# Token layers of a hybrid network: where the first two pairs of the second attention are prepared inside the experts before it

## What is computed

```python
t = t + _L2_attn_ref(_ln_t(t), ...)   # six heads of 16, softmax, the diagonal masked
t = t + _L2_ffn_ref(_ln_t(t), ...)    # four experts 96 -> 384 -> 96, gelu, a gate keeps the best two
t = t + _L3_attn_ref(_ln_t(t), ...)   # six heads of 16, causal
t = t + _L3_ffn_ref(_ln_t(t), ...)    # four experts again
```

## Time and profile before

| | us |
|---|---|
| median of 3 runs | 917.91 |
| lowest and highest | 914.95, 918.13 |
| the profiled execution, its own time | 918.22 |
| span of the profiled execution in the trace | 916.5 |
| PE busy, of the span | 792.8 (86%) |
| ACT busy, of the span | 487.9 (53%) |
| DVE busy, of the span | 548.3 (60%) |
| first experts, parts 6 and 7, on PE | 543.67 to 591.86 |
| first body of the second attention starts on PE | 596.11 |

### The profile page before, as it was taken

How to read it: one execution, slowest core, us unless ns; L and a number is a source line. 1 busy time by engine, 2 the same in 40 slices (tenths; PEclk the granted TensorE clock), 3 DMA queues, 4 the chain that set the end, 5 groups by cost and what they waited for, 6 DMA issues and landing times.

```text
span 916.5 us, 18605 instructions
## 1 busy us (share of the span) xinstructions
PE 792.8 (86%) x6130; PEld 656.2 (72%) x6130; DVE 548.3 (60%) x1632; ACT 487.9 (53%) x777; POOL 320.2 (35%) x365
## 2 busy tenths in 40 slices
PE   1898996899447999889999999789888799999997
PEld 1666664889325677667999998666666688888886
DVE  4799994553626688884555655445777644444442
ACT  0366665111324877775555655447777655555553
POOL 2211112910131444354333344514553553333332
PEclk9999995899758999999999999959999999999999
DMA  4750000000034554510000000344646000000000
GB/s 87 131 101 8 0 0 1 1 0 0 1 79 102 111 112 90 109 22 1 1 1 0 0 0 9 80 94 100 120 92 123 8 1 10 9 9 9 9 9 18
DMA packets 27570, 38.01 MB, mean 41 GB/s; under 512 B 9288, under 2 KB 24352, under 8 KB 27424
## 3 DMA queue, kind: packets, MB, share of 16 engines
q1 hardware_dynamic: 27520, 37.36, 19.7%
HBM read 25.06 MB, written 12.29 MB: 41 GB/s over the span
## 4 chain that ended last, share of the span: by engine, by line
PE 51%; ACT 8%; DVE 5%; DMA 4%; issue 3%; POOL 1%; SPq 1%; ACTq 0%; DVEq 0%; POOLq 0%
PE ps L1331 18%; PE ps L1323 13%; DMA keys<-at_parts 3%; PE ps L1148 3%; PE ps L1170 3%; PE ps L1186 3%; PE ps L1163 2%; ACT at_qs L1456 2%; DVE at_mf L1605 2%; ACT at_pT L1452 2%; PE ps L1213 2%; PE ps L1165 1%; PE ps L1310 1%; PE ps L1192 1%; SPq L1018 1%
## 5 line engine op out<-in xcount | busy, mean ns | idle before, releaser
L1516 ACT ACTIVATE ff_h<-ps,b 128x512 f32<-128x512 f32 x192 | 128.6, 687 | 116.2 <-PE ps L1323 115.8
L1331 PE MATMUL ps<-w,ff_h 128*128 128x96 f32 x1536 | 181.9, 275 | 6.7 <-ACT ff_fT L1522 6.7
L1331 PEld LDWEIGHTS ps<-w,ff_h 128*128 128x128 f32 x1536 | 178.5, 192 | 11.3 <-issue 8.4
L1720 DVE SCALAR_TENSOR_TENSOR tok<-ps,ff_gate,tok 128x96 f32 (+1 forms) x224 | 56.0, 311 | 121.1 <-PE ps L1331 117.0
L1605 DVE TENSOR_REDUCE at_mf<-ps 128x4 f32<-128x1024 f32 (+2 forms) x96 | 100.3, 1081 | 28.1 <-PE ps L1165 27.9
L1058 POOL TENSOR_SCALAR_AFFINE_SELECT at_pT<-at_pT 128x768 f32<-128x768 f32 x64 | 65.8, 1030 | 146.0 <-ACT at_pT L1452 145.4
L1452 ACT ACTIVATE at_pT<-ps 128x1024 f32<-128x1024 f32 (+2 forms) x96 | 87.0, 917 | 22.8 <-PE ps L1170 20.3
L618 DVE SCALAR_TENSOR_TENSOR ca_qk<-ps,dw,ca_qk 96x225 f32<-96x225 f32 (+1 forms) x256 | 97.6, 447 | 2.0 <-ACT ca_qk L467 2.0
L1163 PE MATMUL ps<-keys,at_qs 96*128 96x256 bf16 (+1 forms) x384 | 73.2, 276 | 29.4 <-DMA keys<-at_parts 19.8
L1323 PE MATMUL ps<-ff_xh,ff_wh 96*128 96x512 f32 x192 | 79.7, 415 | 1.3 <-DVE tok L1626 0.9
L1323 PE MATMUL ps<-ff_xh,ff_wl 96*128 96x512 f32 x192 | 75.4, 393 | 0.0
(11 more groups left out here) (231 smaller groups left out, 1529.9 us busy)
## 6 DMA issues: line engine op xcount, KB each, us to landing
at_parts<-at_part SPq DMA_DIRECT2D x96, 96.0 KB
at_qs<-at_parts SPq DMA_DIRECT2D x16, 288.0 KB, 4.3
keys<-at_parts SPq DMA_DIRECT2D x16, 288.0 KB, 5.3
at_qs<-at_parts SPq DMA_DIRECT2D x16, 192.0 KB, 5.8
keys<-at_parts SPq DMA_DIRECT2D x16, 192.0 KB, 6.2
w<-in_L_ffn_w SPq DMA_DIRECT2D x4, 576.0 KB
chan<-in_x SPq DMA_DIRECT2D x4, 384.0 KB, 5.5
at_qs<-at_parts SPq DMA_DIRECT2D x16, 96.0 KB, 6.5
```

Of the source, the lines that this page charges most:

```text
L1331: ins = nc.tensor.matmul(ps[:, 6 + e % 2, C * t:C * (t + 1)], h[:, e % 2, j, P * t:P * (t + 1)], L.f.w2[:, e * HC + j, :], start=(j == 0), ...
L1516: nc.scalar.activation(h[:, e % 2, j, :], ps[:, 3 * (e % 2) + j, :], ACT.Gelu, bias=L.f.b1[:, e * HC + j:e * HC + j + 1]).then_inc(f_h, 1)
```

## The change

The preparation of pairs 8 and 9 moves forward inside parts 6 and 7, on five lists:

- POOL normalises pair 8 in part 5, pair 9 in part 6 and pair 10 in part 7 (`first_experts`), each one part earlier, and ahead of that part's `low` and biases.
- PE transposes the pair after the first `hidden` of its part, into bank 7, once the last `expert` of the part before has left that bank. `queries_keys` stands before `turn_tokens` instead of before the last `result`. There is one more wait, on `s_xT` before `result` of expert 1, which writes bank 7.
- ACT copies `xT` between the gelus of expert 0 and 1. At the end of the part, `high` stands ahead of `tokens_high`, and `middle` of the same pair ahead of the gate's exponential.
- DVE does `rests` before the addition of expert 2 and `lows` before that of expert 3, in the same part.
- SP's list is the same. Its semaphores come earlier.

```diff
@@ POOL
+                def first_experts():
+
+                    part_(L2, 0, True, None)
+                    with pool.Fori(1, PAIRS - 3) as i:
+                        part_(L2, i, True, None)
+                    part_(L2, PAIRS - 3, True, L3.first)
+                    part_(L2, PAIRS - 2, True, L3.first + 1)
+                    part_(L2, PAIRS - 1, False, L3.first + 2)
@@ PE, rest_of_part and part_
                     hidden(L, i, 2)
+                    if pair:
+                        pe.wait_ge(s_xT, pair + 1)
                     result(L, i, 1)
                     hidden(L, i, 3)
                     pe.wait_ge(f_h, i * EH + 3 * HC + 1)
+                    if pair:
+                        queries_keys(L3, pair, pair % 2, qk_bank(pair))
                     if ahead:
                         turn_tokens(i + 1)
-                    if pair == L3.first:
-                        turn(pair, 1)
                     elif pair:
-                        turn(pair, 0)
                         values(L3, pair - 1, 0)
                     result(L, i, 2)
                     if ahead:
                         gate_products(L, i + 1)
-                    if pair:
-                        queries_keys(L3, pair, pair % 2, qk_bank(pair))
                     result(L, i, 3)
...
                     hidden(L, i, 0)
+                    if pair:
+
+                        pe.wait_ge(f_ac, i * E + 2)
+                        turn(pair, 7)
                     hidden(L, i, 1)
@@ ACT, next_part and part_
                     if pair:
-                        normed(pair, pair % 2, 1 if pair == L3.first else 0)
+                        high(pair, qk_bank(pair))
                     if ahead:
                         tokens_high(i + 1)
                     if pair == L3.first + 1:
                         values(pair - 1, 0)
+                    if pair:
+                        middle(pair)
                     if ahead:
                         nc.scalar.preload_act_table(ACT.Exp)
                         gate_exponential(i + 1)
                         nc.scalar.preload_act_table(ACT.Gelu)
-                    if pair:
-                        high(pair, qk_bank(pair))
...
-                        if e == 0 and pair == L3.first + 1:
-                            middle(L3.first)
+                        if e == 0 and pair:
+                            normed(pair, pair % 2, 7)
...
-                middle(L3.first + 1)
@@ DVE, rest_of_part
                     expert(L, i, 1)
-                    if pair == L3.first + 1:
-                        lows(L3.first)
                     add_bias(L, i)
                     if ahead:
                         tokens_turned(i + 1)
+                    if pair:
+                        rests(pair, qk_bank(pair))
                     expert(L, i, 2)
                     if ahead:
                         gate_scores(i + 1)
                     if pair:
-                        rests(pair, qk_bank(pair))
+                        lows(pair)
                     expert(L, i, 3)
...
-                lows(L3.first + 1)
```

More of the change, by code:

```diff
@@ L1125, in _ @@
                 attention(L2)
-                part_(L2, 0, True, None)
-                parts(part_, L2, pool)
-                normed(L3, L3.first + 2)
+                first_experts()
                 attention(L3)
```

## The result

| | before | changed |
|---|---|---|
| median, us | 917.37 (11 runs) | 910.74 (11 runs) |
| lowest and highest | 914.8, 922.42 | 907.05, 913.37 |
| ratio | | 0.9919, 95% interval 0.9897 to 0.9941 |
| the profiled execution's own time | 918.22 | 910.88 |
| its span | 916.5 | 909.1 |

The changed kernel is 0.8% faster, 5.4 to 9.5 us at 917.4. The forecast was 910.7. In one later comparison a single execution of the kernel before took 2710 us; it is left out of the ratios.

The account below looks back on a forecast made before the run. It took PE (86% busy) as the engine to watch, with two waits for POOL, a 4.25 us load wait and a clock dip. -1.32 - 1.47 - 4.25 + 0.1 - 0.3 = -7.2 us gave a median of 910.7; range 904 to 914.

Parts of the forecast that it names:

- The waits and the gap: PE's at_xn waits in parts 6 and 7 (1.32, 1.47 us) and the 4.25 us load wait before the first body go.
- The covers: Parts 5 to 7: reordered POOL, PE, ACT and DVE work fits; cover 3.6 us for low, 1.4 for first gelu; cost nothing.
- What is late next: First body: PE waits 2.9 us for DVE's first maximum; turned maxima 6.3 us after its start; cost 0.1 us, bounds 0 and 1.
- The clock: First two bodies: clock falls inside the first, returns about 5 us into the second; gain 0.3 us, ends 0 and 6.
- The clock line has no 5 there: Sign of being wrong: the page's clock line lacks its 5 around the first two bodies, where half clock was expected.
- The sum: Whole kernel: -1.32 - 1.47 - 4.25 + 0.1 - 0.3 = -7.2 us, median 910.7.
- The first rival: First two bodies: clock stays up or comes back at once, 6 us more gain, about 905 us; chance 0.17.
- The second: Start of part 7 or first body: PE held by the turn_tokens chain or DVE, 3 us lost, 914 us; chance 0.17.
- The third: Second and third bodies: clock stays at 0.50 another body, costing about 8 us or more, 921 us; chance 0.05.

Follow-up runs that it names:

- POOL alone: Kernel before, with only POOL's normalisation of pairs 8, 9 and 10 moved one part earlier; PE, ACT and DVE keep their old order: 911.89 us, ratio 0.9921.
- late casts: Changed kernel with the middle and low parts of pairs 8 and 9 put back to their old places: 913.76 us, ratio 0.9959.
- filled old kernel: Kernel before, with useless matmuls added in the gap ahead of the first body and in three waits of that body: 912.88 us, ratio 0.9956.
- pair 8 alone: Kernel before, with POOL's normalisation of pair 8 alone moved to part 5, pairs 9 and 10 as before: 914.54 us, ratio 0.9979.
- before, body held back: Kernel before, with three useless DVE copies that PE waits for ahead of the second attention's first body: 917.92 us, ratio 1.0006.
- before, statistics later: Kernel before, with DVE's statistics of part 7 moved behind the first body's first three maxima: 917.52 us, ratio 1.0006.
- filled: Changed kernel with useless matmuls in the first body, 24 behind the first scores and 10 behind the transposes that follow: 906.48 us, ratio 0.9862.
- The filled kernels: Kernels with useless matmuls in PE's waits: on the kernel before 912.88 us, on the changed kernel 906.48, on the changed kernel with later statistics 904.55.

## Why the prediction was right

**The waits and the gap.** Forecast -1.32, -1.47 and -4.25, together -7.04, and part 6 at 22.9 and part 7 at 22.4 us. Measured 22.5 and 22.1, and -7.8 up to the first body. The mechanism is shown piece by piece. POOL alone removes both `at_xn` waits, and late casts bring a gap back (5.94 us). The three terms do not stand alone, though: the second wait is worth something only together with the early casts. Of the 0.8 us more, 0.5 lie in part 6 and 0.3 in part 7. A gap of 0.16 us at the end of part 6 is gone, and the two results of part 7 now stand together (one row of 48 matmuls); what the rest is was not tested.

**The covers.** Costed at nothing, and they cost nothing. `low` of part 7 ends at 562.85 + 1.27 = 564.1 and the part starts at 567.25, a cover of 3.1 us against 3.6 forecast. ACT waits 1.17 us for PE at the first gelu, against 1.4 forecast. In part 5 POOL normalises pair 8 until 540.0 and `low` starts at 540.29, as soon as its input is there: POOL was free 0.29 us before, as tight as forecast. The timeline of POOL in the changed kernel has both:

```profile
539.17 0.83 POOL L855 TENSOR_TENSOR at_xn<-at_xn,rstd 128x384 f32<-128x384 f32 x1 [0.18 <-POOL at_xn L851]
540.29 1.26 POOL L1071 TENSOR_TENSOR ff_xl<-ff_xT,ff_xh 96x512 fp32r<-96x512 f32 x1 [0.29 <-ACT ff_xh L1483]
...
562.85 1.27 POOL L1071 TENSOR_TENSOR ff_xl<-ff_xT,ff_xh 96x512 fp32r<-96x512 f32 x1 [2.48 <-ACT ff_xh L1483]
```

**What is late next.** The wait for the first maximum was forecast at 2.9 us and is 2.81. The distance to the turned maxima was under-sized: 6.3 forecast, 7.7 and 7.5 measured, since the scores behind the wait ran at half clock (1.45 us against 0.7) and 1.24 us and not 0.5 passed from the end of the third maximum (594.83 + 0.96) to the turned maxima, 0.85 of them in a copy of DVE. The term of +0.1 is +1.0 in one pair of profiles (7.50 - 6.48) and +1.4 in the other. It is the term that was mis-sized.

**The clock.** Forecast -0.3 with ends of 0 and -6. The two bodies came out at -1.0 in one pair of profiles and +1.0 in the other (36.2 against 35.2). Less the term above, the clock's own part is -2.4 in the one and 0 in the other. The fall some microseconds into the first body is in both profiles (+3.6 and +4.0). The return about 5 us into the second body is in the second alone (5.3 us); in the first it comes 1.4 us ahead of that body. "The clock line has no 5 there" was a sign of being wrong. The first page has a 6 there, so by this sign the forecast of the return failed in that execution, while the page of the second has the 5.

**The sum.** To the end of the second body the forecast is -7.2, and the two pairs give -8.8 and -6.8 us. In the first pair 1.5 us come back in stretches that the change does not touch, so that its spans differ by 7.4. The waits and the gap are shown. That the number is within a microsecond of the measured 6.6 (7.4 by the ratio) is partly luck: the terms are off by 0.8, by 0.9 to 1.3 and by up to 2.1 us, with both signs.

**The rivals.** The first rival, the clock staying up, did not happen, but its price was about right: both bodies at full clock were put at 29 us and take 29.1 and 29.0 where the waits are filled. The second did not occur at its price of 3 us, though the longer way to the turned maxima is a piece of it. The third did not occur, and 8 us for a body more at half clock looks too high: 20.5 us of half clock instead of 13.6 made the two bodies of the changed kernel 2.1 us longer.

**What stays open.** POOL alone gave 7.3 us (4.7 to 9.9), though its body starts only 1.8 us sooner. Its pair of profiles explains 4.8 us, at the edge of the interval. The fall in part 7 of the filled old kernel is no help: in the old order it lies in the shadow of the loads. The records of the single runs do help. Each has the mean granted clock of the execution, and as the clock has two levels, the time at half clock is twice the share that is missing, times the span. In every kernel the longer runs have more of it (914.3 us at 0.952 and 921.7 at 0.941 for the kernel before beside POOL alone). A line through all 181 such runs, each kernel about its own mean, has 0.28 us of time for each microsecond at half clock. Means at half clock over the whole execution, in us:

| kernel | its runs | the kernel before beside it |
|---|---|---|
| POOL alone | 82.2 | 99.7 |
| pair 8 alone | 91.7 | 97.1 |
| before, filled | 78.4 | 97.1 |
| before, body held back | 96.5 | 98.0 |
| before, statistics later | 99.6 | 98.0 |

The changed kernel has 92.0, and filled 77.8. The 17.5 us less of POOL alone are worth some 5 us by that line (an estimate), and with the 1.8 us they make up the 7.3. So its surplus goes with less time at half clock, but no run shows why this order has less of it. The last two kernels have no less than before beyond the scatter: their profiles, with 13.6 and 13.7 us, do not stand for their runs.

## What to carry to other kernels

A preparation that ends in a store and a reload has its deadline one reload before its use, so it is the last cast, not the first product, that has to move; find it as the instruction ahead of the DMA in the chain of waits. When a long wait goes, list what the other engines did in its shadow: here DVE's statistics, harmless before (1.0006 when moved), came to stand in a 2.8 us wait, and moving them in the changed kernel gave 3.4 us more. Compare times over many executions: the first two bodies of one kernel differed by 2 us between two profiles, and its runs by 8. And before a single profile is taken to explain a time, compare its mean granted clock with that of the other runs.

## What the runs showed of the hardware

The granted clock in and just ahead of the first two bodies was low for 0, 6.8, 10.2, 13.6, 20.5 or 23.9 us in fourteen profiles of nearly the same work, and it stayed low through stretches in which PE's rows were busy (0.50 with 2.00 of 2.00 us busy in 604 to 606 of the kernel before). With the same work the first two bodies took 32.1 us where the fall lay some 2 us ahead of the first, and 35.1 where it lay 0.4 us ahead; the kernel with the body held back by 1.0 us showed the shorter, and so did one with the body at its old place (32.3). A microsecond at half clock went with 0.28 us of time over the runs, where a half of such a microsecond is the most that PE can lose in it. The Trainium skill, "TensorE: Matmul & The Clock Gate", section "What's actually happening", says that activity releases the throttle. The filled kernels agree, for with the waits filled it stayed up through both bodies (29.1 and 29.0 us). The kernels without filler agree only in part, since in them it came back late in spite of matmuls close behind each other. The wait of 1.5 us for `at_xn` inside the otherwise dense part 7 was followed by a low clock in one of the six profiles that have it.
